# A four-sublayer transformer kernel: the ternary FFN runs once over 512 tokens, and its two square weights share one buffer

## The chip, the cores and the metric

The kernel runs on one core of one Trainium2 chip, in one launch. The metric is the device time of that launch in microseconds, as a median over runs. A run's time is that of the whole launch; the profile shows one execution, and its span reaches from the first to the last instruction.

## The reference

The input x is 16 sequences (tiles) of 512 tokens with 256 features. Four sublayers follow each other, each on a layer norm of x and added back to x:

```python
x = x + L0_attn(layernorm(x))   # linear attention: phi(q) (phi(k)^T v), 16 heads, output projection
x = x + L0_ffn(layernorm(x))    # h = silu(x w1) * (x w2); h = gelu(h h1); h = gelu(h h2); h w3
x = x + L1_attn(layernorm(x))   # softmax(q k^T / 16) v, one head of 256, output projection
x = x + L1_ffn(layernorm(x))    # tanh(x W A1 A2 + bias)
```

The hidden width of L0_ffn is 1024: w1 and w2 are 256 x 1024, h1 and h2 are 1024 x 1024, w3 is 1024 x 256. These five weights hold only -1, 0 and 1, with one scale for each output column.

## The kernel before

Precision: a float32 product is made of fp32r matmuls. An operand is split into a high part (`_hi`) and the rest (`_lo`). The ternary weights are exact in the high part, so an FFN product takes two matmuls (weight x hi, weight x lo); all other products take three (`product3`).

Work is written as steps. A step has a kind, a number and an owner (the letter ahead of the colon), and each engine has its own queue of steps, written out by hand in `PE_ORDERS`, `DVE_ORDERS`, `ACT_ORDERS` and `POOL_ORDERS`, with a part FIRST (the start and tile 0), a part BODY that is walked 14 times, and a part END. `a` and `b` behind a step cut it in two, so that other steps come between. An engine does its queue strictly in order. The engines meet through semaphores: `full` and `taken` of the four PSUM banks in each of two rings (`ffn_fill` for the FFN, `att_fill` for the rest), and counters such as `ffn_ready`, `xt_lo_ready`, `xn_ready`.

The steps that matter here:
- AST, BST, CST, DST: layer-norm statistics on DVE (bn_stats, bn_aggr, adding epsilon), with the inverse root on POOL (L631). ANO, BNO, CNO, DNO: the normalisation on DVE (L686).
- T: DVE transposes the normalised tile by 32 x 32 blocks into `turned` (L764), ACT copies it to `xt_hi` (L953), POOL subtracts to `xt_lo` (L654). LT does the same through TensorE (L1136), ACT (L949) and DVE (L754). NT and NTL are the DVE transposition of half a tile for the FFN (L779, L961, L786).
- U0 to U3 (w1, w2, silu, product), G0 to G3 (h1, gelu), H0 to H3 (h2, gelu), W (w3): the FFN for half a tile of 256 tokens. One step makes two blocks of 128 hidden columns, each 256 tokens wide, in one bank. So a tile takes two passes, and in BODY there are two runs of U, G, H and W: one of the second half of a tile, one of the first half of the next.
- AKV, AS, AQ, AM, AO: the linear attention. Owner `a`.
- CV, CZ, CS0 to CS3, CP0 to CP3, CO0 to CO3, CF: the softmax attention and the last sublayer. CS is a product of scores, then a row maximum on DVE (L869), two small operations (L872, L875), and an exponential on ACT (L1009). CP transposes the probabilities on TensorE (L1252). Owner `c`.

TensorE fills a bank for G or H with 32 matmuls of 256 columns (`hidden`, L1117); U takes 32 for its two banks (`product`, L1048); W is 32 matmuls of 256 columns (L1174). The next layer waits block by block: G0 (and H0, W) waits for `ffn_ready` of the block pair that it reads. All five weights stay in SBUF for the whole run. x has four slots.

ACT's gelu, exponential and silu stand in different tables. Where the function changes, the compiler puts an ACT_TABLE_LOAD ahead of the ACTIVATE.

Of the kernel before, what the change touches and what calls it, by code (L numbers as in the profile page):

```python
# [136 lines left out]
def steps_from(plan):  # L137
# [13 lines left out]
    U0 c:CST U1 U2 U3 c:CNO G0 c:LT c:CB c:CQ G1 c:CV c:CZ G2 c:CS0 G3 c:CP0 c:CS1 c:CS2 c:CO0 c:CP1 c:CS3  # L151
    H0 c:CO1 c:CP2 H1 c:CO2 BST1 c:CP3 BNO1 a:AST H2 c:CO3 c:DST H3 NT1 NTL1 c:DNO W0 c:LT a:ANO U0 U1 c:CF a:T
    U2 U3 a:AB a:AKV0 a:AKV1 a:AKV2 G0 a:AKV3 G1 G2 a:AS a:AQ a:AM G3 a:AO H0 H1 n:BST0 n:BNO0 H2 H3 n:NT0 n:NTL0
    W1""")
# [65 lines left out]
def before(value):  # L220
# [5 lines left out]
    WARM24 p:AST p:ANO p:AB PREP0 p:LT p:AKV0 SCALE p:AKV1 p:AKV2 p:AKV3 PREP1 p:AS f:FA0 p:AQ a:AST f:FA1 p:AM f:FA2  # L226
    f:TA0 p:AO a:ANO a:LT LOOK00 LOOK01 f:TA1 m:BST0 a:AKV0 a:AKV1 f:TA2 m:BNO0 m:BT0 CHECK0
    U0 U1 U2 U3 LOOK10 a:AB LOOK11 a:AKV2 LOOK12 a:AKV3 LOOK13 CHECK1 a:AS a:AQ
    G0 a:AM G1 a:AO WIDE G2 LOOK20 LOOK21 FOLD0 TAKE0 G3 LOOK22 LOOK23 CHECK2 LOOK30
    H0 CHECK3 H1 BST1 BNO1 H2 H3 BT1 W0 U0 U1 U2 U3 G0 G1 G2 G3 H0 H1 n:BST0 n:BNO0 H2 H3 n:NT0 n:NTL0 W1""")  # L230
BODY = PLAN
END = steps_from("""
    U0 U1 U2 U3 G0 G1 G2 G3 H0 H1 BST1 BNO1 H2 H3 BT1 W0 U0 U1 U2 U3 G0 G1 G2 G3 H0 H1 c:CST c:CNO H2 c:LT H3 c:CB W1
    d:CST c:CQ c:CV c:CZ d:CNO d:LT c:CS0 c:CS1 d:CB d:CQ d:CV c:CP0 c:CO0 d:CZ c:CP1 c:CO1 c:CS2 c:CS3
    d:CS0 d:CS1 c:CP2 c:CO2 c:CP3 c:CO3 d:CP0 d:CO0 c:DST d:CS2 d:CP1 d:ES0 d:CO1 d:EN0 c:DNO d:CS3 d:ET0 c:LT d:ES1 d:EN1
    d:CP2 d:EF0 c:CF d:CO2 d:ET1 d:EF1 d:ES2 d:CP3 d:EN2 d:CO3 d:ES3 d:ET2 d:EF2 d:EN3 d:ET3 d:EF3""")


def order_from(plan):
# [21 lines left out]
    p:AST p:ANO PREP0 p:LT p:AKV0 SCALE p:AKV1 p:AKV2 a:ASTa p:AKV3 a:ASTb PREP1 f:TA0 p:AS p:AQ p:AM LOOK00  # L261
    a:ANO LOOK01 p:AO a:LT m:BST0 f:TA1 CHECK0 m:BNO0 f:TA2 a:AKV0 m:BT0 a:AKV1 a:AKV2 a:AKV3 U0 LOOK10
    LOOK11 LOOK12 a:AS LOOK13 a:AQ CHECK1 U1 U2 a:AM U3 a:AO LOOK20 WIDE G0 LOOK21 G1 LOOK22 LOOK23 TAKE0
    CHECK2 LOOK30 G2 G3 CHECK3 BST1 BNO1 H0 H1 n:BST0 H2 H3 BT1 W0 U0 U1 U2 U3 n:BNO0 n:NT0a G0 n:NT0b G1 G2
    n:NTL0 G3 H0 H1 H2 H3 W1"""),
# [5 lines left out]
    "END": order_from("""  # L271
    U0 U1 U2 U3 G0 G1 G2 G3 BST1 BNO1 H0 H1 H2 H3 BT1 W0 U0 U1 U2 U3 G0 G1 G2 G3 c:CST c:CNO H0 c:LT H1 c:CQ
    H2 H3 W1 d:CST c:CV d:CNO c:CZ d:LT c:CS0 c:CS1 d:CQ c:CP0 d:CV d:CZ c:CO0 c:CP1 d:CS0 c:CO1 c:CS2 c:CS3
    d:CS1 c:CP2 d:CP0 c:CO2 c:CP3 d:CO0 d:CS2 d:ES0 c:CO3 d:CP1 c:DSTa d:EN0 c:DSTb d:CO1 d:CS3 d:ET0 d:ES1
    d:CP2 d:EN1 c:DNO d:EF0 d:CO2 d:ET1 c:LT d:CP3 d:EF1 d:ES2 c:CF d:EN2 d:CO3 d:ES3 d:ET2 d:EN3 d:EF2
    d:ET3 d:EF3"""),
# [1092 lines left out]
```

## Time and profile before

| what | value |
|---|---|
| median of 3 runs | 1983.03 us (1981.29 to 1983.25) |
| span of the profiled execution | 1981.5 us |
| mean granted TensorE clock | 0.996 |
| busy: PE, DVE, ACT, POOL | 1961.9, 1289.0, 1020.0, 406.8 us |
| one walk of BODY | 120.64 us |
| DMA moved, mean | 46.03 MB, 23 GB/s |

The profile has no time of its own for the profiled launch besides the span; the span is 1.5 us under the median of the runs. In rows, times are microseconds from the start of the span. Matmuls overlap in their records, so the spacing of matmuls is read from the chain, which counts no microsecond twice.

### The profile page before, as it was taken

To read this page: it belongs to the slowest core of one execution; us is meant where nothing else is said; L and a number is where in the kernel's file an instruction comes from. 1 tells how busy PE (TensorE), PEld (TensorE's weight loads), DVE (VectorE), ACT (ScalarE), POOL (GpSimd) and SP (SyncE) were. 2 spreads that over 40 slices of the span, in tenths; PEclk is the share of its full clock that TensorE was granted. 3 is DMA by queue.
4 is the path that set the end of the run, shared out by engine and by line. 5 is a ranking of instruction groups with operands and counts; after the bars stand their busy time and mean duration, and the time that the engine had idled before them with its cause. 6 is when DMAs were issued, how large, how long until landed. Compare 5 with 4: busy or idle time off the path is not lost.

```text
span 1981.5 us, 37810 instructions
## 1 busy us (share of the span) xinstructions
PE 1961.9 (99%) x15288; PEld 1895.6 (96%) x15288; DVE 1289.0 (65%) x3292; ACT 1020.0 (51%) x1786; POOL 406.8 (21%) x344
## 2 busy tenths in 40 slices
...
DMA packets 24538, 46.03 MB, mean 23 GB/s; under 512 B 1264, under 2 KB 21488, under 8 KB 24176
## 3 DMA queue, kind: packets, MB, share of 16 engines
...
## 4 chain that ended last, share of the span: by engine, by line
PE 97%; DMA 1%; DVE 1%; SPq 1%; issue 0%; ACT 0%; POOL 0%; DVEq 0%; ACTq 0%
PE ffn_fill L1117 49%; PE att_fill L1048 25%; PE ffn_fill L1048 13%; PE ffn_fill L1174 6%; PE att_fill L1136 1%; PE att_fill L1252 1%; DMA scratch_w2T<-in_w2T 1%; DMA w<-scratch_w1T 0%; SPq L543 0%; PE ffn_fill L1285 0%; DVE late_sm L869 0%; PE ffn_fill L1280 0%; ACT late_kv_b L1009 0%; DVE st L671 0%; DVE late_prob_t_lo L864 0%
## 5 line engine op out<-in xcount | busy, mean ns | idle before, releaser
L1117 PE MATMUL ffn_fill<-act_hi,h 128*128 128x256 f32 x4096 | 987.2, 283 | 0.8 <-issue 0.2
L1117 PE MATMUL ffn_fill<-act_lo,h 128*128 128x256 f32 x4096 | 978.2, 280 | 1.2 <-issue 1.2
L1117 PEld LDWEIGHTS ffn_fill<-act_hi,h 128*128 128x128 f32 x4096 | 770.3, 188 | 9.2 <-POOL act_lo L649 3.9
L1117 PEld LDWEIGHTS ffn_fill<-act_lo,h 128*128 128x128 f32 x4096 | 773.1, 189 | 3.6
L976 ACT ACTIVATE whole<-ffn_fill,scales 128x256 f32<-128x256 f32 x512 | 214.0, 469 | 291.3 <-PE ffn_fill L1117 290.1
L649 POOL TENSOR_TENSOR act_lo<-whole,act_hi 128x512 fp32r<-128x512 f32 x128 | 166.8, 1303 | 492.4 <-DVE act_hi L798 492.4
L802 DVE TENSOR_TENSOR act_lo<-whole,act_hi 128x512 fp32r<-128x512 f32 x256 | 183.4, 716 | 112.0 <-ACT act_hi L980 109.7
L1048 PE MATMUL ffn_fill<-half_hi,w 128*128 128x256 f32 x1024 | 245.9, 283 | 0.0
L1048 PE MATMUL ffn_fill<-half_lo,w 128*128 128x256 f32 x1024 | 244.3, 281 | 0.0
L1048 PEld LDWEIGHTS ffn_fill<-half_lo,w 128*128 128x128 f32 x1024 | 193.3, 189 | 0.1
L1048 PEld LDWEIGHTS ffn_fill<-half_hi,w 128*128 128x128 f32 x1024 | 192.5, 188 | 0.4 <-issue 0.2
L631 POOL TENSOR_TENSOR rstd_B<-var_eps_B,minus_half 128x2 f32<-128x2 f32 x32 | 27.8, 868 | 776.4 <-DVE var_eps_B L680 776.4
L967 ACT ACTIVATE gated<-ffn_fill,scales 128x256 f32<-128x256 f32 x256 | 107.3, 471 | 140.4 <-PE ffn_fill L1048 137.3
L980 ACT ACTIVATE act_hi<-whole 128x512 fp32r<-128x512 f32 x256 | 161.9, 633 | 8.1
L976 ACT ACT_TABLE_LOAD x102 | 130.9, 1283 | 59.7 <-PE ffn_fill L1117 58.7
L779 DVE STREAM_TRANSPOSE turned_b<-xn_b 32x128 f32<-32x128 f32 x464 | 140.4, 303 | 6.5
L793 DVE SCALAR_TENSOR_TENSOR whole<-ffn_fill,scales,gated 128x256 f32<-128x256 f32 x256 | 111.8, 478 | 50.3 <-PE ffn_fill L1048 29.3
L1174 PE MATMUL ffn_fill<-w,act_hi 128*128 128x256 f32 x512 | 121.2, 280 | 0.0
L1174 PE MATMUL ffn_fill<-w,act_lo 128*128 128x256 f32 x512 | 120.9, 279 | 0.0
L764 DVE STREAM_TRANSPOSE turned<-xn 32x256 f32<-32x256 f32 x224 | 97.5, 435 | 2.9
L1174 PEld LDWEIGHTS ffn_fill<-w,act_lo 128*128 128x128 f32 x512 | 96.5, 188 | 0.0
L671 DVE BATCH_NORM_STATS2 st<-x 128x6 f32<-128x256 f32 x252 | 92.7, 415 | 5.8 <-DMA x<-in_L_attn_x 4.3
...
## 6 DMA issues: line engine op xcount, KB each, us to landing
x<-in_L_attn_x SPq DMA_DIRECT2D x16, 512.0 KB, 3.3
out<-x SPq DMA_DIRECT2D x15, 512.0 KB, 2.9
...
```

The lines of the kernel that those rows point to most:

```text
L649: pool.tensor_tensor(act_lo[0][:, blocks], whole[:, n % WHOLES], act_hi[0][:, blocks].bitcast(F32), ALU.subtract).then_inc(s["ffn_ready"], 1)
L671: last = dve.bn_stats(st[:, b, :], xs[:, b, :])
L764: last = dve.transpose(into[:, :, :, here:here + SQ], own.xn[here:here + SQ].rearrange("p b (k n) -> p b k n", k=KD) [:, :, :, there:there ...
L779: last = dve.transpose(into[:, :, :, here:here + SQ], xn_b[here:here + SQ].rearrange("p b (k n) -> p b k n", k=KD) [:, :, :, there:there + ...
L793: last = dve.scalar_tensor_tensor(whole[:, n % WHOLES, o, :], two(bank)[:, o, :], scales[:, 1, 2 * j + o:2 * j + o + 1], gated[:, j % 2, o ...
L802: dve.tensor_tensor(act_lo[dst][:, blocks], whole[:, n % WHOLES], act_hi[dst][:, blocks].bitcast(F32), ALU.subtract).then_inc(s["ffn_ready ...
L967: last = act.activation(gated[:, j % 2, o, :], two(bank)[:, o, :], ACT.Silu, scale=scales[:, 0, 2 * j + o:2 * j + o + 1])
L976: last = act.activation(whole[:, n % WHOLES, o, :], two(bank)[:, o, :], ACT.Gelu, scale=scales[:, layer, 2 * j + o:2 * j + o + 1])
L980: act.activation(act_hi[1 if kind == "G" else 0][:, 2 * j:2 * j + 2], whole[:, n % WHOLES], ACT.Copy)\
L1048: last = pe.matmul(out, lhsT, rhs, start=n == 0, stop=n == len(pairs) - 1)
L1117: last = pe.matmul(two(bank)[:, o, :], view(w), view(moving[:, k, :]), start=k == 0 and o == 0 and half == 0, stop=k == KH - 1 and half == ...
L1174: last = pe.matmul(bank[:, 0:D], view(part_of[:, k, b * P:(b + 1) * P]), view(w3[:, k, :]), start=k == 0 and half == 0, stop=k == KH - 1 a ...
```

## The change

The FFN of a tile runs once over 512 tokens. U, G and H have eight steps each; a step makes one block of 128 hidden columns, 512 tokens wide, with matmuls of 512 columns. W stays as it is, as W0 and W1 back to back. `h1` and `h2` no longer lie side by side in SBUF. One buffer `hw` of eight chunks holds one of them; when TensorE has filled G_j's bank, SP loads chunk j of h2 into its place, and behind H_j chunk j of h1. x has three slots instead of four. The probabilities, w3 and some raw weights lie elsewhere, with two pads of eight elements. All queues are new, SP has one of its own, and a walk of BODY now begins in the middle of layer H. ACT's U0 and U1 have one wait more, since W's product now goes through `gated`.

```diff
-SLOTS = 4
+SLOTS = 3
 PE_ORDERS "BODY"
-    U0 U1 U2 U3 G0 G1a c:LT G1b c:CV c:CZ G2a c:CS0 G2b G3a c:CP0 c:CS1 c:CS2 G3b c:CO0 c:CP1 c:CS3 H0a
-    c:CO1 c:CP2 H0b c:CO2 c:CP3 H1 c:CO3 H2 H3 W0 U0 c:LT U1 U2 U3 c:CFa G0a c:CFb G0b G1 G2 G3 a:AKV0
-    a:AKV1 a:AKV2 a:AKV3 H0a a:AS a:AQ a:AM H0b H1a a:AO H1b H2 H3 W1"""),
+         H5 H6 H7 W0 W1 U0 a:AKV0 U1 a:AKV1 U2 a:AKV2 U3 a:AKV3 U4 U5 a:AS a:AQ U6 a:AM U7 G0a a:AO G0b c:LT G1a
+    c:CV     G1b c:CZ G2 c:CS0 G3a c:CP0 c:CS1 c:CS2 G3b c:CO0 c:CP1 c:CS3 G4a c:CO1 c:CP2 G4b c:CO2 c:CP3 G5
+    c:CO3 G6     G7a c:LT G7b H0a c:CFa H0b c:CFb H1 H2 H3 H4"""),
 DVE_ORDERS "BODY"
-    c:CSTa U0 U1 U2 U3 c:CSTb c:CNO c:LT c:CQ c:CV c:CZ c:CS0 G0 c:CP0 c:CS1 c:CS2 c:CO0 G1 c:CP1 c:CS3 G2
-    G3 c:CO1 c:CP2 c:CO2 BST1 c:CP3 H0 BNO1 a:AST c:CO3 c:DSTa H1 c:DSTb NT1a H2 NT1b H3 NTL1 c:DNO W0 U0 U1
-    c:LT U2 U3 a:ANO c:CF a:Ta a:Tb G0 G1 a:AKV0 a:AKV1 G2 a:AKV2 a:AKV3 a:AS G3 a:AQ a:AM a:AO n:BST0 H0
-    n:BNO0 H1 n:NT0a H2 n:NT0b H3 n:NTL0 W1"""),
+         H5 a:AST H6 a:ANO a:Ta H7 a:Tb W0 W1 c:CSTa U0 a:AKV0 U1 a:AKV1 c:CSTb U2 a:AKV2 U3 a:AKV3 U4 U5 a:AS
+    a:AQ U6 a:AM U7 c:CNO a:AO n:BST0 c:LT c:CQ G0 n:BST1 c:CV G1 c:CZ c:CS0 G2 c:CP0 c:CS1 c:CS2 c:CO0 G3
+    c:CP1 c:CS3 c:CO1 c:CP2 G4 c:CO2 c:CP3 n:BNO0 c:CO3 G5 c:DSTa c:DSTb n:NT0a G6 c:DNO n:NT0b c:LT G7 n:NTL0
+    n:BNO1     c:CF H0 n:NT1a H1 n:NT1b H2 n:NTL1 H3 H4"""),
 ACT_ORDERS "BODY"
-    U0 U1 U2 U3 c:LT G0 G1 c:CV c:CZ c:CS0 c:CP0 G2 c:CS1 c:CS2 c:CP1 G3 c:CS3 c:CP2 H0 c:CP3 H1 H2 H3 NT1
-    U0 U1 c:LT U2 U3 c:CF G0 a:T G1 G2 a:AKV0 a:AKV1 a:AKV2 a:AKV3 G3 a:AQ a:AM H0 H1 H2 H3 n:NT0"""),
+         H5 H6 H7 a:T U0 a:AKV0 U1 a:AKV1 U2 a:AKV2 U3 a:AKV3 U4 U5 a:AQ U6 a:AM U7 G0 c:LT G1 c:CV c:CZ G2
+    c:CS0 c:CP0 c:CS1 c:CS2 G3 c:CP1 c:CS3 c:CP2 G4 c:CP3 G5 G6 c:LT n:NT0 G7 H0 c:CF H1 H2 n:NT1 H3 H4"""),
 POOL_ORDERS "BODY"
-    U0 U1 U2 U3 c:CST c:CB BST1 a:AST c:DST U0 U1 U2 U3 c:CF a:T a:AB n:BST0"""),
+         a:AST a:AB a:T U0 U1 c:CST U2 U3 U4 U5 U6 U7 n:BST0 c:CB n:BST1 c:DST c:CF"""),
+SP_ORDERS "BODY"
+    H5 H6 H7 G0 G1 G2 G3 G4 G5 G6 G7 H0 H1 c:CF H2 H3 H4"""),
...
-        h1 = sb("h1", [P, KH, HID], F32R)
-        h2 = sb("h2", [P, KH, HID], F32R)
+        hw = sb("hw", [P, KH, KH, P], F32R)
...
+            def land_chunk(name, j):
+                sp.dma_start(hw[:, j].rearrange("p k n -> p (k n)").bitcast(F32), a["scratch_" + name][j])\
+                  .then_inc(h_loaded[j], 16)
...
+                if kind in ("G", "H"):
+                    b, n = c.bank("ffn_fill", 0)
+                    sp.wait_ge(full["ffn_fill"][b], n)
+                    land_chunk("h2T" if kind == "G" else "h1T", j)
...
+                elif kind == "CF":
+                    t = c.now.get("out_ready", 0)
+                    sp.wait_ge(s["out_ready"], t + 1)
                     sp.dma_start(x_out[t], x[:, t % SLOTS]).then_inc(x_stored, 16)
+                    if t + SLOTS < T:
+                        sp.wait_ge(x_stored, 16 * t + 16)
+                        sp.dma_start(x[:, t % SLOTS], x_in[t + SLOTS]).then_inc(x_loaded[t % SLOTS], 16)
...
                 elif kind == "U":
                     if j >= 2:
                         wait_taken(act, c, "ffn_fill", -3)
+                    else:
+                        wait(act, s["b_done"], c.value("b_done", j - 1))
                     bank, out = filled(act, c, "ffn_fill", 0)
-                    for o in range(2):
-                        last = act.activation(gated[:, j % 2, o, :], two(bank)[:, o, :], ACT.Silu,
-                                              scale=scales[:, 0, 2 * j + o:2 * j + o + 1])
-                    last.then_inc(out, 1)
+                    act.activation(gated[:, j % 2], bank[:], ACT.Silu, scale=scales[:, 0, j:j + 1]).then_inc(out, 1)
...
-            def hidden(c, layer, weights, src, j, piece):
+            def hidden(c, layer, src, j, piece):
                 bank, done = begun(c, "ffn_fill", piece)
+                if piece != "b":
+                    pe.wait_ge(h_loaded[j], weights_loaded(c))
                 def emit(view):
                     for k in halves(piece, KH):
-                        if j == 0 and k % 2 == 0:
-                            pe.wait_ge(s["ffn_ready"], c.value("ffn_ready", k // 2 + 1 - PAIRS))
-                        for o in range(2):
-                            w = weights[:, k, (2 * j + o) * P:(2 * j + o + 1) * P]
-                            for half, moving in enumerate((act_hi[src], act_lo[src])):
-                                last = pe.matmul(two(bank)[:, o, :], view(w), view(moving[:, k, :]),
...
+                        if j == 0:
+                            pe.wait_ge(s["ffn_ready"], c.value("ffn_ready", k + 1 - KH))
+                        for half, moving in enumerate((act_hi[src], act_lo[src])):
+                            last = pe.matmul(bank[:], view(hw[:, j, k, :]), view(moving[:, k, :]),
+                                             start=k == 0 and half == 0, stop=k == KH - 1 and half == 1)
```

In FIRST, tile 0 now has both m:BT0 and m:BT1 (transposition through TensorE for the FFN) ahead of U0, with m:BT1 directly ahead of it.

## Rows read from the trace of the kernel before

**Rows 1.** The page, busy time: us, share of the span, instructions.
```profile
PE 1961.9 (99%) x15288; PEld 1895.6 (96%) x15288; DVE 1289.0 (65%) x3292; ACT 1020.0 (51%) x1786; POOL 406.8 (21%) x344
```

**Rows 2.** Stretches: one walk of BODY, and a part of END; PEclk is the granted clock.
```profile
300.00:420.64 120.64, 120.61 (x950) 117.05 (x949) 80.81 (x208) 64.28 (x112) 25.82 (x21) 1.00 0.03 10
...
1919.00:1945.00 26.00, 24.73 (x151) 21.36 (x149) 21.39 (x54) 11.27 (x21) 6.02 (x5) 1.00 0.00 1
```

**Rows 3.** The chain in BODY, in order of time: start, us, what, matmuls.
```profile
340.50 13.25 PE ffn_fill L1117 x112
353.74 5.60 PE att_fill L1048 x24
...
373.35 9.46 PE ffn_fill L1117 x80
382.80 3.73 PE ffn_fill L1174 x32
...
400.07 0.87 PE att_fill L1136 x8
...
410.31 1.43 PE att_fill L1048 x6
```

**Rows 4.** The timeline, DVE: start, us, line, operation.
```profile
310.44 0.16 DVE L881 RECIPROCAL sm<-sm 128x1 f32<-128x1 f32 x1 [1.79 <-PE att_fill L1048]
...
311.04 0.74 DVE L671 BATCH_NORM_STATS2 st<-x 128x6 f32<-128x256 f32 x2
...
314.20 1.40 DVE L671 BATCH_NORM_STATS2 st<-x 128x6 f32<-128x256 f32 x4
...
316.12 0.16 DVE L881 RECIPROCAL sm<-sm 128x1 f32<-128x1 f32 x1
...
319.37 2.50 DVE L779 STREAM_TRANSPOSE turned_b<-xn_b 32x128 f32<-32x128 f32 x8
321.89 0.69 DVE L802 TENSOR_TENSOR act_lo<-whole,act_hi 128x512 fp32r<-128x512 f32 x1
...
326.48 1.37 DVE L686 TENSOR_SCALAR xn<-x,mv_C,rstd_C 128x256 f32<-128x256 f32 x4
...
341.14 7.17 DVE L764 STREAM_TRANSPOSE turned<-xn 32x256 f32<-32x256 f32 x16
```

**Rows 5.** The timeline, ACT and DVE, behind the last H step of a pass.
```profile
382.90 0.84 ACT L976 ACTIVATE whole<-ffn_fill,scales 128x256 f32<-128x256 f32 x2 [2.28 <-PE ffn_fill L1117]
383.77 0.63 ACT L980 ACTIVATE act_hi<-whole 128x512 fp32r<-128x512 f32 x1
...
384.44 0.69 DVE L802 TENSOR_TENSOR act_lo<-whole,act_hi 128x512 fp32r<-128x512 f32 x1 [0.53 <-ACT act_hi L980]
```

**Rows 6.** The timeline, ACT and POOL, behind the transposition T.
```profile
348.35 1.16 ACT L953 ACTIVATE xt_hi<-turned 128x512 fp32r<-128x512 f32 x2 [3.08 <-DVE turned L764]
...
349.06 2.54 POOL L654 TENSOR_TENSOR xt_lo<-turned,xt_hi 128x512 fp32r<-128x512 f32 x2 [5.36 <-ACT xt_hi L953]
```

**Rows 7.** The timeline, ACT and DVE, behind c:LT.
```profile
400.55 1.09 ACT L949 ACTIVATE xt_hi<-att_fill 128x512 fp32r<-128x512 f32 x2 [6.45 <-PE att_fill L1136]
...
401.25 1.29 DVE L754 TENSOR_TENSOR xt_lo<-att_fill,xt_hi 128x512 fp32r<-128x512 f32 x2 [1.73 <-ACT xt_hi L949]
```

**Rows 8.** The timeline, DVE and ACT, behind c:CS0.
```profile
411.77 0.69 DVE L869 TENSOR_REDUCE sm<-att_fill 128x1 f32<-128x512 f32 x1 [1.76 <-PE att_fill L1048]
...
412.99 1.28 ACT L1009 ACT_TABLE_LOAD   x1 [3.83 <-DVE sm L875]
414.28 0.69 ACT L1009 ACTIVATE kv_b<-att_fill,sm 128x512 f32<-128x512 f32 x1
```

**Rows 9.** Groups of ACT by line, 300 to 1800 us: busy, mean ns, idle before and releaser.
```profile
L976 ACT ACT_TABLE_LOAD x87 | 111.6, 1283 | 36.4 <-PE ffn_fill L1117 35.6
```

**Rows 10.** DMA issues: operation and count, KB each, us from issue to landing.
```profile
x<-in_L_attn_x SPq DMA_DIRECT2D x16, 512.0 KB, 3.3
```

**Rows 11.** The chain while the weights still land.
```profile
44.96 3.84 PE ffn_fill L1048 x32
```

More of the change, by code:

```diff
@@ L46 @@
 HB = HT // P
-PAIRS = KH // 2
-SLOTS = 4
+SLOTS = 3
 WHOLES = 2
@@ L150 @@
 PLAN = steps_from("""
[L151 to L154, printed above, removed]
+    H5 a:AST H6 H7 a:ANO W0 a:AB a:T W1 U0 c:CST a:AKV0 U1 a:AKV1 U2 a:AKV2 U3 a:AKV3 U4 U5 a:AS a:AQ U6 a:AM U7
+    c:CNO a:AO n:BST0 G0 c:LT G1 G2 G3 G4 G5 c:CB c:CQ n:BST1 c:CV c:CZ c:CS0 c:CP0 c:CS1 c:CS2 c:CO0 c:CP1
+    c:CS3 c:CO1 c:CP2 c:CO2 c:CP3 n:BNO0 c:CO3 c:DST n:NT0 G6 c:DNO c:LT G7 n:NTL0 n:BNO1 c:CF H0 n:NT1 H1 H2
+    n:NTL1 H3 H4""")
 def only(*whose):
     return [s for s in PLAN if s[2] in whose]
-CHECKED = ["w12", "h1", "h2", "w3"]
+CHECKED = ["w12", "h1", "h2a", "h2b", "h2c", "h2d", "w3"]
+H1, H2 = CHECKED.index("h1"), CHECKED.index("h2a")
 def total(steps):
@@ L225 @@
 FIRST = steps_from("""
[L226 to L230, printed above, removed]
+    WARM24 p:AST p:ANO p:LT PREP0 p:AKV0 p:AKV1 SCALE p:AKV2 a:AST p:AKV3 f:FA0 PREP1 p:AB p:AS f:TA0 p:AQ p:AM
+    LOOK00 f:FA1 a:ANO LOOK01 p:AO a:LT m:BST0 f:FA2 m:BST1 f:TA1 m:BNO0 a:AKV0 CHECK0 f:TA2 m:BT0 m:BNO1 a:AKV1
+    a:AKV2 a:AKV3 m:BT1 U0 LOOK10 U1 U2 LOOK11 a:AS LOOK12 a:AQ LOOK13 U3 a:AB U4 U5 CHECK1 a:AM U6 WIDE U7 a:AO
+    n:BST0 G0 n:BST1 G1 G2 LOOK20 G3 n:BNO0 FOLD0 TAKE0 G4 CHECK2 LOOK30 G5 n:NT0 G6 CHECK3 LOOK40 n:NTL0 G7
+    n:BNO1 H0 CHECK4 LOOK50 LOOK60 H1 CHECK5 H2 CHECK6 n:NT1 H3 n:NTL1 H4""")
 BODY = PLAN
 END = steps_from("""
[L233 to L236, printed above, removed]
+    o:H5 o:H6 o:H7 o:W0 o:W1 U0 U1 U2 U3 U4 U5 U6 U7 G0 G1 G2 G3 G4 G5 G6 G7 H0 H1 H2 c:CST H3 c:CNO H4 H5 c:LT
+    H6 H7 c:CB W0 W1 d:CST c:CQ c:CV c:CZ d:CNO d:LT c:CS0 c:CS1 d:CB d:CQ d:CV c:CP0 c:CO0 d:CZ c:CP1 c:CO1
+    c:CS2 c:CS3 d:CS0 d:CS1 c:CP2 c:CO2 c:CP3 c:CO3 d:CP0 d:CO0 c:DST d:CS2 d:CP1 d:ES0 d:CO1 d:EN0 c:DNO d:CS3
+    d:ET0 c:LT d:ES1 d:EN1 d:CP2 d:EF0 c:CF d:CO2 d:ET1 d:EF1 d:ES2 d:CP3 d:EN2 d:CO3 d:ES3 d:ET2 d:EF2 d:EN3
+    d:ET3 d:EF3""")
 def order_from(plan):
@@ L260 @@
     "FIRST": order_from("""
[L261 to L265, printed above, removed]
+         p:AST p:ANO PREP0 p:LT p:AKV0 SCALE p:AKV1 p:AKV2 a:ASTa p:AKV3 a:ASTb PREP1 f:TA0 p:AS p:AQ p:AM
@@ L266 @@
+    LOOK00     a:ANO LOOK01 p:AO a:LT m:BST0 m:BST1 f:TA1 CHECK0 m:BNO0 f:TA2 a:AKV0 m:BT0 m:BNO1 a:AKV1 a:AKV2
+    a:AKV3 m:BT1     U0 LOOK10 U1 U2 LOOK11 a:AS LOOK12 LOOK13 a:AQ U3 U4 U5 CHECK1 a:AM U6 WIDE U7 a:AO n:BST0
+    n:BST1 G0 G1 G2 LOOK20     G3 TAKE0 n:BNO0 G4 CHECK2 LOOK30 G5 n:NT0a G6 CHECK3 LOOK40 n:NT0b n:NTL0 n:BNO1
+    G7 CHECK4 LOOK50 LOOK60 H0     CHECK5 CHECK6 n:NT1a H1 n:NT1b H2 n:NTL1 H3 H4"""),
     "BODY": order_from("""
-    c:CSTa U0 U1 U2 U3 c:CSTb c:CNO c:LT c:CQ c:CV c:CZ c:CS0 G0 c:CP0 c:CS1 c:CS2 c:CO0 G1 c:CP1 c:CS3 G2
@@ L271 @@
+    n:BNO1     c:CF H0 n:NT1a H1 n:NT1b H2 n:NTL1 H3 H4"""),
     "END": order_from("""
[L272 to L275, printed above, removed]
@@ L276 @@
-    d:ET3 d:EF3"""),
+         o:H5 o:H6 o:H7 o:W0 o:W1 U0 U1 U2 U3 U4 U5 U6 U7 G0 G1 G2 G3 G4 G5 G6 G7 H0 H1 H2 c:CST H3 c:CNO H4 H5
+    c:LT H6     c:CQ H7 W0 W1 d:CST c:CV d:CNO c:CZ d:LT c:CS0 c:CS1 d:CQ c:CP0 d:CV d:CZ c:CO0 c:CP1 d:CS0
+    c:CO1 c:CS2 c:CS3     d:CS1 c:CP2 d:CP0 c:CO2 c:CP3 d:CO0 d:CS2 d:ES0 c:CO3 d:CP1 c:DSTa d:EN0 c:DSTb d:CO1
+    d:CS3 d:ET0 d:ES1     d:CP2 d:EN1 c:DNO d:EF0 d:CO2 d:ET1 c:LT d:CP3 d:EF1 d:ES2 c:CF d:EN2 d:CO3 d:ES3
+    d:ET2 d:EN3 d:EF2     d:ET3 d:EF3"""),
@@ L292 @@
     "FIRST": order_from("""
-    p:AST a:AST p:AB m:BST0 U0 U1 U2 U3 a:AB BST1 U0 U1 U2 U3 n:BST0"""),
+         p:AST a:AST p:AB m:BST0 m:BST1 U0 U1 U2 a:AB U3 U4 U5 U6 U7 n:BST0 n:BST1"""),
     "BODY": order_from("""
-    U0 U1 U2 U3 c:CST c:CB BST1 a:AST c:DST U0 U1 U2 U3 c:CF a:T a:AB n:BST0"""),
+         a:AST a:AB a:T U0 U1 c:CST U2 U3 U4 U5 U6 U7 n:BST0 c:CB n:BST1 c:DST c:CF"""),
     "END": order_from("""
-    U0 U1 U2 U3 BST1 U0 U1 U2 U3 c:CST d:CST d:CB c:CB d:ES0 c:DST d:ES1 d:EF0 d:EF1 d:ES2 c:CF d:ES3 d:EF2
+         U0 U1 U2 U3 U4 U5 U6 U7 c:CST d:CST d:CB c:CB d:ES0 c:DST d:ES1 d:EF0 d:EF1 d:ES2 c:CF d:ES3 d:EF2
     d:EF3"""),
+}
+SP_ORDERS = {
+    "FIRST": order_from("""
+    G0 G1 G2 G3 FOLD0 G4 G5 G6 G7 H0 H1 H2 H3 H4"""),
+    "BODY": order_from("""
+    H5 H6 H7 G0 G1 G2 G3 G4 G5 G6 G7 H0 H1 c:CF H2 H3 H4"""),
+    "END": order_from("""
+    o:H5 o:H6 o:H7 G0 G1 G2 G3 G4 G5 G6 G7 c:CF d:EF0 d:EF1 d:EF2 d:EF3"""),
 }
@@ new lines, in _ @@
+            sp.dma_start(x[:, 1], x_in[1]).then_inc(x_loaded[1], 16)
+            bounce(w12_bounced, "w1T")
+            bounce(w12_bounced, "w2T")
+            bounce(h1_bounced, "h1T", 0)
+            sp.wait_ge(w12_bounced[0], 16 * 2)
+            land(w12_loaded[0], "w1T", w12[:, 0])
+            land(w12_loaded[1], "w2T", w12[:, 1])
+            bounce(h1_bounced, "h1T", 1)
+            for half in range(2):
+                sp.wait_ge(h1_bounced[half], 16)
+                for j in range(half * KH // 2, (half + 1) * KH // 2):
+                    land_chunk("h1T", j)
@@ L702, in part @@
                     wait(dve, s["turned"], c.value("turned"))
-                    normalise(c, own, x[:, slots[who]], own.xn, "A" if kind == "ANO" else "E" if who == "d" else "C", NB)
+                    stage, of_kind = ("A", "AST") if kind == "ANO" else ("E" if who == "d" else "C", "CST" if kind == "CNO" else "DST")
+                    normalise(c, own, x[:, slots[who]], own.xn, stage, pow_of(c, own, of_kind, 0, who), range(NB))
                 elif kind == "CQ":
@@ L717, in part @@
                     wait_apart(dve, taken[own.ring][b], n)
-                    statistics(c, own, x[:, slots[who]], stage_of(step), NB, share)
+                    statistics(c, own, x[:, slots[who]], stage_of(step), range(NB), share)
                 elif kind == "ES":
```

316 lines of the change are left out of this document (157 added, 159 removed).

## Prediction

> **What bounds the kernel now.** I read the page first: TensorE is busy 1961.9 of 1981.5 us, and no other engine is over 65% [rows 1]. Then the stretches: in one walk of BODY TensorE is busy 120.61 of 120.64 us at a granted clock of 1.00, its upper level of 2.4 GHz [rows 2]. So 14 x 120.64 = 1689 us of the span hold no wait of TensorE at all. Two things can move the time: what a matmul costs, and whether the new queues let TensorE wait. The chain gives the first, the timeline of the other engines the second. The sum is made against the span, 1981.5; the runs' median is 1.5 us above it, and I add that at the end. A difference under 0.2%, 4 us, can't be told from none.
>
> **The matmuls.** 112 matmuls of 256 columns take 13.25 us, 118.3 ns each; 24 of 512 columns take 5.60 us, 233.3 ns each [rows 3]. Two narrow ones cost 236.6 ns, so the change saves 3.3 ns for each wide one. A tile has 64 + 128 + 128 = 320 of these (U, G, H): 1.05 us a tile, 16.7 us for 16 tiles. W is unchanged. The bounds: W's 32 matmuls of 256 columns take 3.73 us, 116.6 ns each [rows 3], which is half of 233.3. So the 1.7 ns that G pays over W may not be the price of a short matmul but of where its operands lie, and may stay at 512 columns. Then the gain is 0. I take 16.7, because the only rows with 512 columns show 233.3, and keep 0 for the range. The Trainium skill ("TensorE: Matmul & The Clock Gate", section "Wait — 56ns, not 53.3ns?") gives each warm matmul a fixed cost of about 2.5 ns; by it the gain would be an estimated 16 x 320 x 2.5 = 12.8 us, 4 less.
>
> **ACT, DVE, POOL: the same elements in fewer instructions.** A gelu that was two records in 0.84 us [rows 5] becomes one of 512 columns; the exponential of 512 columns takes 0.69 [rows 8]. All of this lies under TensorE's matmuls and is worth nothing by itself; it shortens the way from a full bank to DVE's subtraction from 384.44 - 382.81 = 1.63 us [rows 3, 5] to 1.48.
>
> **SP and the chunks.** 16 loads of 512 KB a tile, where x's of that size lands in 3.3 us [rows 10]. A chunk is needed eight steps later, at least 8 x 3.73 = 30 us: hidden. x's load now waits for c:CF and the store, after H1 in SP's queue, behind which only loads of chunks wait. It lands before the walk ends, and a:AST needs it 5.2 us into the next: hidden too, at three slots. Bound: while the weights landed, U's matmuls took 3.84 / 32 = 120.0 ns [rows 11], 1.4% more. If that is the DMA's doing, and a chunk is on its way for 16 x 3.3 = 53 us of a walk, it costs 0.7 us a tile, 12 us in all. I take 0.
>
> **The queues.** Without waits a walk lasts 120.64 - 1.05 = 119.6 us. A G or H step is 16 x 233.3 ns = 3.73 us, half of one 1.87, a U step 1.87. I followed the new queues through BODY with durations from the rows, and find four places where TensorE gets there first:
>
> 1. *a:T before AKV0.* Count from the start of H5. TensorE comes to AKV0 after H5, H6, H7, W0, W1, U0: 5 x 3.73 + 1.87 = 20.5. H6 is full at 7.47, its subtraction starts at 8.95. Behind it DVE has the subtraction (0.69), a:ANO (1.37), Ta (half of 7.17), H7 (0.69) and Tb [rows 4], all in order: 18.9. From T's end to xt_lo ACT and POOL take 351.60 - 348.31 = 3.3 us [rows 4, 6]. AKV0 can start at 22.2. **1.6 us**, half of which shows already in W0, which needs H7's block at 14.5 and gets it at 15.3. W's own two steps on DVE, the release of U0's banks, c:CST and U0 are queued behind Tb and still make it. Before, four G steps lay between T and AKV0.
> 2. *G0 ahead of c:LT on ACT.* Count from G0's full bank, where TensorE starts c:LT. ACT's wait for the bank stands ahead of its table load [rows 9], so G0 takes load 1.29, gelu 0.71, copy about 0.6 [rows 5, 8]: c:LT's copy starts at 2.7. From there DVE starts 0.70 later and gives the first bank back after 0.65 more [rows 7]: 4.05. TensorE has LT (0.87) and G1a (1.87) to do, 2.74, then CV. **1.3 us.** Behind c:LT on ACT stand only G1 and CV.
> 3. *One half step between CS0 and CP0.* From CS0's end (411.74) to the exponential's end (414.97) the row maximum, the table load and the exponential take 3.23 us [rows 3, 8]. Before, G2b and G3a covered it with 3.78; now G3a alone with 1.87. **1.4 us.**
> 4. *DNO before the second c:LT.* Count from CO3's end. DVE: CO3 0.64, G5 0.69, c:DST 1.92, n:NT0a 2.52, G6 0.69, DNO 1.37 [rows 4], 7.8 in all, and 0.2 for the last two transposes: 8.05. TensorE: G6, G7a, LT, 6.47 [rows 3]. **1.6 us.** n:NT0b and c:LT's subtraction wait behind DNO on DVE; CFa, which needs them, comes 0.9 us after.
>
> Elsewhere the walk fits: AM to AO, CP to CO, G7 to H0, the H steps with n:NT1. All four are in places where the waited-for engine is not busy on average, so nothing is given back. Sum: 5.9 us a walk, 14 walks, 82.9 us. Bounds: 0 if each chain is shorter than I read it; one more place like these, 1.4 x 14 = 20 us.
>
> For places 2 and 3 the table load matters. The rows have it at 1.28, and the exponential starts 1.29 after it began [rows 8]. The Trainium skill ("ScalarE: Activation LUTs", section "What ACT_TABLE_LOAD costs") adds about 1380 ns of drain to each switch; places 2 and 3 would then last 2 x 1.38 us longer, 39 us over the run, a time of about 2089. The row has no room for that drain, so I go by the row.
>
> **FIRST and END.** m:BT1 directly ahead of U0 shows its way through ACT and DVE once: about 0.67 + 0.69 = 1.4 us [rows 5]. The other steps of FIRST and END are the same work on TensorE, without attention beside most of it; 0, and 5 us either way for the range.
>
> **Sum.** 1981.5 - 16.7 + 82.9 + 1.4 = 2049.1 span; with 1.5 around it 2050.6 us. Slower by 3.4%.
>
> **Rivals.**
> - *The table loads go ahead of the wait in the new queues* (the compiler places them). Then places 2 and 3 shrink by 1.28 each to about 0.1 and nothing: 2050.6 - 14 x 2.6 = 2014 us. Against it: G's and CS's waits are as they were, and 35.6 of the 36.4 us of idle time ahead of gelu's loads is put down to TensorE [rows 9]. 0.13.
> - *The wait chains overlap more than I read*, because every block could be handed on before its step ends, and the places together cost under (16.7 - 1.4) / 14 = 1.1 us a walk: from there on the kernel is faster. At 0 it gives 1968 us. For it: rows of DVE overlap by up to 0.08 us, which takes some 0.1 off each place; against it: that is far from 1.5. 0.09.
> - *The wide matmuls are quicker in the FFN than in AKV*, where hi and lo weights alternate. From 220 ns down they pay for all waits (5120 of them, 84.3 us); at N / 2.4 GHz plus 2.5 ns, 215.8, the gain is 320 x 20.8 ns = 6.7 us a tile, 107 us: 1961 us. That this is what 512 columns take is the rule of the same TensorE page. Against it: AKV's are 233.3 at the same granted clock [rows 2, 3], and the narrow ones are as far above the rule (118.3). 0.04.
> - *Nothing gained by width, or the chunks' DMA slows the matmuls, or one more place.* 2067 to 2083 us. For it: W's 116.6 and rows 11. 0.19.
> - *The waits lower TensorE's clock.* In END it stood idle for 1.3 of 26 us at a granted clock of 1.00 [rows 2]; waits of 1.3 to 1.6 us are of that order. It would go far above 2083. 0.02.
> - *The change does nothing*, since waits and gain cancel: the narrow zone around 1.1 us a walk. 0.03.
>
> **How the numbers follow.** My forecast, the four places at 1.0 to 1.7 us each with the full gain, has 0.50, and 2030 to 2062 as its own range. Faster: 0.09 + 0.04 = 0.13. Same: 0.03. Slower: 0.84. The range takes in the table-load rival at the bottom and the bounds of width and DMA at the top, and leaves out the faster cases and the clock: 2008 to 2080.
>
> **What would show it.** In the page: TensorE busy about 83 us less than the span beyond the old 20, and its waits on POOL xt_lo, on DVE xt_lo (CV), on ACT kv_b (CP0) and on DVE xn (LT), 14 times each. The spacing in U, G, H at 233.3 ns and half as many matmuls there. In the stretches a walk of 125.5 us. If the walk is 119 to 121 us with no such waits, my following of the queues failed; if waits stand there but at a third of the size, the durations did; if the spacing is not 233, the first term.

## The result, and the profile after

The changed kernel takes 2039.53 us (4 runs, 2039.30 to 2040.71) beside 1983.14 us for the kernel before in the same runs: 2.85% slower, 95% interval 2.7% to 3.0%. The forecast was 2050 us in 2008 to 2080. The span of the profiled execution is 2037.9 us. Two single executions were far slower at a granted clock of 0.72 and 0.70 (one of the kernel before, 2462.69 us, and one of e8, 3391.75 us) and count nowhere here.

The page of the changed kernel, busy time (us, share of the span, instructions) and the DMA issues:

```profile
PE 1926.6 (95%) x10170; PEld 1632.2 (80%) x10170; DVE 1328.5 (65%) x3183; ACT 817.7 (40%) x1286; POOL 409.8 (20%) x344
...
hw<-scratch_h1T SPq DMA_DIRECT2D x128, 512.0 KB, 3.3
hw<-scratch_h2T SPq DMA_DIRECT2D x128, 512.0 KB, 3.2
```

TensorE is busy 35 us less than in [rows 1] and yet the span is 56 us longer: its idle time went from 20 to 111 us. So the loss is waiting, 91 us more of it, less the 35 us of work saved. Who it waited for (line of the waiting matmul, releaser, us in total, times, longest):

```profile
PE att_fill L1170 <- DVE xn L720: 24.5, 16, 4.2
PE att_fill L1283 <- ACT kv_b L1044: 22.3, 15, 1.6
PE att_fill L1083 <- DVE xt_lo L791: 20.2, 15, 1.4
PE att_fill L1083 <- POOL xt_lo L686: 14.2, 14, 1.0
PE ffn_fill L1205 <- DVE act_lo L840: 13.1, 14, 0.9
```

These are the four places of the prediction: c:LT for DNO, CP0 for the exponential of CS0, CV for c:LT's xt_lo, and AKV0 for T, the last with its forerunner in W0. Each stands there 14 times, once for each walk of BODY, or once or twice more: the 4.2 us of the first line, for one, fell in FIRST. Two walks of BODY in a row (stretch, us; busy time of PE, PEld, DVE, ACT, POOL; granted clock, DMA share, GB/s):

```profile
899.60:1024.60 125.00, 118.74 (x629) 100.64 (x629) 83.17 (x201) 50.66 (x80) 26.04 (x21) 1.00 0.23 76
1024.60:1149.60 125.00, 118.76 (x629) 100.62 (x629) 83.13 (x201) 50.64 (x80) 26.03 (x21) 1.00 0.23 76
```

A walk takes 125.00 us instead of 120.64 [rows 2], with 6.2 us of idle TensorE where there were 0.03. The granted clock stayed at 1.00 with these waits in the walk. The same walk in the timeline of TensorE, only the matmuls that waited (start, duration, in brackets the idle time ahead):

```profile
933.98 0.38 PE L1083 MATMUL att_fill<-wvo_hi,xt_hi 128*128 128x256 f32 x1 [1.34 <-DVE xt_lo L791]
...
949.97 0.33 PE L1283 MATMUL att_fill<-ident,kv_b 128*128 128x128 f32 x1 [1.57 <-ACT kv_b L1044]
...
978.01 1.31 PE L1170 MATMUL att_fill<-ident,xn 128*128 128x128 f32 x8 [1.39 <-DVE xn L720]
...
1017.25 0.39 PE L1205 MATMUL ffn_fill<-w,act_hi 128*128 128x256 f32 x1 [0.94 <-DVE act_lo L840]
...
1024.60 0.50 PE L1083 MATMUL att_fill<-wkv_hi,xt_hi 128*128 128x512 f32 x1 [1.02 <-POOL xt_lo L686]
```

They sum to 6.26 us. DVE's queue ahead of the last two shows place 1 as it was followed:

```profile
1010.90 0.69 DVE L840 TENSOR_TENSOR act_lo<-whole,act_hi 128x512 fp32r<-128x512 f32 x1 [1.00 <-ACT act_hi L1015]
1011.50 1.38 DVE L720 TENSOR_SCALAR xn<-x,mv_A,rstd_A 128x256 f32<-128x256 f32 x4
1012.91 3.58 DVE L801 STREAM_TRANSPOSE turned<-xn 32x256 f32<-32x256 f32 x8
1016.50 0.69 DVE L840 TENSOR_TENSOR act_lo<-whole,act_hi 128x512 fp32r<-128x512 f32 x1
1017.23 3.60 DVE L801 STREAM_TRANSPOSE turned<-xn 32x256 f32<-32x256 f32 x8
```

H6's subtraction starts at 1010.90, then a:ANO, Ta, H7, Tb end at 1020.83, and POOL gives xt_lo back 3.7 us later. For place 2, ACT behind G0's full bank:

```profile
930.00 1.28 ACT L1013 ACT_TABLE_LOAD   x1 [6.68 <-PE ffn_fill L1152]
931.29 0.69 ACT L1013 ACTIVATE whole<-ffn_fill,scales 128x512 f32<-128x512 f32 x1
932.01 0.63 ACT L1015 ACTIVATE act_hi<-whole 128x512 fp32r<-128x512 f32 x1
932.55 1.06 ACT L988 ACTIVATE xt_hi<-att_fill 128x512 fp32r<-128x512 f32 x2
```

ACT had been idle for 6.68 us, and the table load still came only behind the bank, which was full at 929.93; c:LT's copy starts 2.62 us after that, against the 2.7 of the forecast.

What the prediction did not have is the pace of the matmuls. The chain of the changed kernel (start, us, what, matmuls):

```profile
938.89 2.72 PE att_fill L1083 x12
...
946.63 0.70 DVE sm L908
947.36 0.23 DVE sm L911
947.61 0.17 DVE sm L914
947.85 1.28 ACT L1044
949.14 0.79 ACT kv_b L1044 x2
949.97 0.66 PE att_fill L1283 x4
...
956.61 0.44 PE att_fill L1283 x4
...
978.01 1.31 PE att_fill L1170 x8
...
987.63 21.80 PE ffn_fill L1152 x96
```

96 matmuls of H1 to H6 take 21.80 us: 227.1 ns each, not 233.3 [rows 3]. CZ's 12 take 2.72, 226.7 ns, and nothing in the order or width of CZ's matmuls was changed.

Behind a wait the chain gives a group of matmuls more time than without one: CP0's four transposes take 0.66 us after the wait for ACT, and those of CP1 at 956.61 take 0.44. The ends of matmul records are modelled, so how this splits into waiting and slow work is rough; the starts are not, and from start to start AKV0's first matmul takes 0.33 us and the second 0.24:

```profile
1024.60 0.50 PE L1083 MATMUL att_fill<-wkv_hi,xt_hi 128*128 128x512 f32 x1 [1.02 <-POOL xt_lo L686]
1024.93 0.40 PE L1083 MATMUL att_fill<-wkv_lo,xt_hi 128*128 128x512 f32 x1
1025.17 0.39 PE L1083 MATMUL att_fill<-wkv_hi,xt_lo 128*128 128x512 f32 x1
```

c:LT's eight transposes take 1.31 us instead of 0.87 [rows 3] for another reason: in the kernel each pair of them waits for its own quarter of DNO, and DVE was still at work on these while TensorE transposed:

```profile
977.46 1.38 DVE L720 TENSOR_SCALAR xn<-x,mv_C,rstd_C 128x256 f32<-128x256 f32 x4
978.01 1.31 PE L1170 MATMUL att_fill<-ident,xn 128*128 128x128 f32 x8 [1.39 <-DVE xn L720]
```

DNO ends at 978.84, and the last pair can't start before that. So c:LT waits for DNO by 0.44 us more than the 1.39 that stand in brackets.

### The profile page after: what moved, and what is told of

It reads as the page before. It is cut to its first block, busy times and chain, and to the rows that moved or that the text cites. A ratio compares the mean times of both kernels' runs of the same rounds, so it can differ in the third digit from the quotient of the medians.

```text
span 2037.9 us, 27407 instructions
## 1 busy us (share of the span) xinstructions
PE 1926.6 (95%) x10170; PEld 1632.2 (80%) x10170; DVE 1328.5 (65%) x3183; ACT 817.7 (40%) x1286; POOL 409.8 (20%) x344
## 2 busy tenths in 40 slices
DMA packets 59241, 171.10 MB, mean 84 GB/s; under 512 B 5296, under 2 KB 25520, under 8 KB 58928
## 4 chain that ended last, share of the span: by engine, by line
PE 76%; DVE 13%; ACT 5%; POOL 2%; issue 2%; DMA 1%; SPq 1%; ACTq 0%; DVEq 0%
PE ffn_fill L1152 37%; PE att_fill L1083 25%; PE ffn_fill L1083 11%; DVE turned L801 5%; POOL xt_lo L686 2%; DVE turned_b L818 2%; DVE act_lo L840 2%; PE att_fill L1283 1%; DVE xn L720 1%; DVE st L704 1%; PE att_fill L1170 1%; ACT whole L1013 1%; ACT L1044 1%; ACT act_hi L1015 1%; ACT L1013 1%
## 5 line engine op out<-in xcount | busy, mean ns | idle before, releaser
L1152 PE MATMUL ffn_fill<-act_hi,hw 128*128 128x512 f32 x2048 | 804.0, 393 | 1.3 <-DVE act_lo L840 1.3
L1152 PE MATMUL ffn_fill<-act_lo,hw 128*128 128x512 f32 x2048 | 798.7, 390 | 0.0
L1152 PEld LDWEIGHTS ffn_fill<-act_hi,hw 128*128 128x128 f32 x2048 | 384.7, 188 | 78.4 <-DVE act_lo L840 1.8
L1152 PEld LDWEIGHTS ffn_fill<-act_lo,hw 128*128 128x128 f32 x2048 | 384.7, 188 | 76.8
L1013 ACT ACTIVATE whole<-ffn_fill,scales 128x512 f32<-128x512 f32 x256 | 175.9, 687 | 526.9 <-PE ffn_fill L1152 526.4
L1083 PE MATMUL ffn_fill<-half_hi,w 128*128 128x512 f32 x512 | 202.6, 396 | 2.3 <-issue 2.3
L1083 PE MATMUL ffn_fill<-half_lo,w 128*128 128x512 f32 x512 | 199.8, 390 | 0.0
L1083 PEld LDWEIGHTS ffn_fill<-half_hi,w 128*128 128x128 f32 x512 | 96.1, 188 | 22.2 <-issue 2.5
L1083 PEld LDWEIGHTS ffn_fill<-half_lo,w 128*128 128x128 f32 x512 | 96.1, 188 | 19.7
L1205 PEld LDWEIGHTS ffn_fill<-w,act_hi 128*128 128x128 f32 x512 | 96.3, 188 | 16.6 <-DVE act_lo L840 16.0
```

The source lines that it names most:

```text
L1013: act.activation(whole[:, n % WHOLES], bank[:], ACT.Gelu, scale=scales[:, layer, j:j + 1]).then_inc(out, 1)
L1083: last = pe.matmul(out, lhsT, rhs, start=n == 0, stop=n == len(pairs) - 1)
L1152: last = pe.matmul(bank[:], view(hw[:, j, k, :]), view(moving[:, k, :]), start=k == 0 and half == 0, stop=k == KH - 1 and half == 1)
L1205: last = pe.matmul(bank[:, 0:D], view(part_of[:, k, tok]), view(w3[:, k, :]), start=k == 0 and half == 0, stop=k == KH - 1 and half == 1)
```

## The experiments

All times are medians of 4 runs (of three for e8), and ratios are against the kernel before, run beside each group (medians 1983.0 to 1985.0 us). Eleven kernels ran.

**Where the 227 ns come from.** The changed kernel has two pads of 8 elements, 32 bytes. The starts of the operands follow from the order and the sizes of the tensors in the kernel. In the kernel before, the start of each weight lies on a multiple of 64 bytes and that of each activation 32 bytes behind one. In the changed kernel the operands of U, G, H, AKV, AQ, CZ and CS all start on a multiple of 64, and w3, wvo, wf, m_parts and the high part of the values 32 bytes off. Run e1 takes the pads out:

```diff
-        sb("beside_0", [P, 8])
-        sb("beside_1", [P, 8])
```

> The changed kernel without its two pads of eight elements. It computes the reference. Theory A: the new kernel's wide matmuls run at 227 ns instead of the 233.3 of before because the pads put both operands of U, G, H, AKV, AQ and CZ in the same half of a 64-byte line; without them one operand lies 32 bytes off, and these go back to 233.3 ns, CO and AO (both operands at 32) to 119.2 ns. That is 5120 + 770 wide matmuls x 6.4 ns = 38 us and 3 us for the narrow ones, less some 12 us because a slower TensorE waits less at two of the four places: about 2068 us. Rival B: 227 ns comes from the width or the order of the steps, not from where the operands lie: 2039 us and 227 ns.

Measured: 2068.47 us, 1.0429 (1.0411 to 1.0448). The chain of e1 has layer H and AO as

```profile
1001.74 22.41 PE ffn_fill L1150 x96
...
938.83 2.86 PE att_fill L1081 x24
```

22.41 / 96 = 233.4 ns, and AO's 24 narrow ones 119.2 ns each. Theory A, and within 1 us of its time.

Run e2 does it to the kernel before:

```diff
+        sb("beside_0", [P, 8])
         scales = sb("scales", [P, 4, KH])
```

> The kernel before with one pad of eight elements ahead of the scales, so that the activations lie on 64-byte lines like the weights. It computes the reference. Theory A: what counts is whether both operands lie in the same half of a line, and it has opposite signs for wide and narrow matmuls: AKV, AQ, CZ go from 233.3 to 227 ns (5 us less), U, G, H from 118.3 to 119.2 ns and W, CV, CF from 116.6 to 119.2 ns (about 14 us more): about 1992 us. Rival B: where operands lie does nothing: 1983 us. Rival C: it is the activations' own place at 32 bytes off a line that costs, at any width: G below 117 ns and 1965 us or less.

Measured: 2000.56 us, 1.0088 (1.0070 to 1.0106). The chain of e2:

```profile
952.19 13.44 PE ffn_fill L1118 x112
965.63 5.47 PE att_fill L1049 x24
```

The 112 narrow matmuls go from 118.3 to 120.0 ns and AKV's 24 wide ones from 233.3 to 227.9, opposite signs as in theory A. The narrow ones lose more than the 0.9 ns that I had put in: 10240 in the FFN x 1.7 ns is 17 us.

Run e9 moves everything by 32 bytes:

```diff
+        sb("ahead", [P, 8])
         w12 = sb("w12", [P, 2, KD, HID], F32R)
```

> The changed kernel with one more pad of eight elements ahead of the first tensor: everything moves by 32 bytes, so that operands which shared the first half of a 64-byte line now share the second. It computes the reference. Theory A (only the distance of the two operands counts): 227 ns in U, G, H and 2039.5 us. Rival B (the absolute place counts, 64-byte alignment is fast): 233 ns and about 2068 us.

Measured: 2040.47 us, 1.0286 (1.0269 to 1.0303), and in its chain

```profile
988.80 21.80 PE ffn_fill L1153 x96
```

227.1 ns. Of A and B it is A: the distance between the two operands counts, and a shift of both by 32 bytes does nothing. How far the rule reaches is not shown. In all these kernels the operands "in the same half" are also a whole number of 256 bytes apart, and the others 32 bytes more or less, so nothing here says that the period is 64 bytes.

The kernel before had one group of wide matmuls of this kind, the scores CS, whose two operands are both activations:

```profile
410.42 0.39 PE L1048 MATMUL att_fill<-xt_lo,qz_hi 128*128 128x512 f32 x1
...
411.34 0.40 PE L1048 MATMUL att_fill<-xt_hi,qz_lo 128*128 128x512 f32 x1
```

These are four matmuls from start to start, 0.92 us, 230 ns each: under 233.3, though not 227.

**Whether the four places are the loss.** Run e3 rearranges the queues there and nowhere else (each line shows one stretch of an engine's queue, before and after, the rest cut):

```diff
 DVE  -H5 a:AST H6 a:ANO a:Ta H7 a:Tb W0            +a:AST H5 a:ANO a:Ta H6 H7 a:Tb W0
      -c:CZ c:CS0 G2 c:CP0 c:CS1 c:CS2 c:CO0 G3     +c:CZ c:CS0 c:CP0 c:CS1 c:CS2 c:CO0 G2
      -c:CP1 c:CS3 c:CO1                            +c:CP1 c:CS3 G3 c:CO1
      -c:DSTb n:NT0a G6 c:DNO n:NT0b c:LT G7        +c:DSTb c:DNO n:NT0a c:LT G6 G7 n:NT0b
 ACT  -U7 G0 c:LT G1 c:CV c:CZ G2 c:CS0 c:CP0       +U7 c:LT G0 c:CV G1 c:CZ c:CS0 c:CP0
      -c:CS1 c:CS2 G3 c:CP1                         +c:CS1 c:CS2 G2 c:CP1 G3
      -G6 c:LT n:NT0 G7                             +G6 c:LT G7 n:NT0
 PE   -c:CZ G2 c:CS0 G3a c:CP0                      +c:CZ G2a c:CS0 G2b G3a c:CP0
```

> The changed kernel with its BODY queues rearranged at the four places only (T ahead of H6 and H7 on DVE with its statistics ahead of H5; c:LT ahead of G0 on ACT; a whole step between CS0 and CP0, with G2 behind CS2 on ACT; DNO ahead of NT0a, and NT0b and n:NT0 behind G7). It computes the reference. Theory: TensorE's 6.2 us of idle time per walk of BODY and the slower first matmuls behind each wait (1.2 us) stand at these places alone, so nearly all of it goes: 14 x 7.2 = 100 us less, 1940 us, below the kernel before, with at most 0.3 us idle per walk. Rival: the engines are late for lack of slack anywhere in the walk, and the waits come back at other steps: 2010 us or more.

Measured: 1942.04 us, 0.9794 (0.9776 to 0.9812): 97.5 us less than the changed kernel, and faster than the kernel before. One walk of e3, and its largest wait:

```profile
974.30:1092.27 117.97, 117.67 (x629) 100.71 (x629) 84.06 (x201) 50.99 (x80) 25.88 (x21) 1.00 0.24 81
...
PE att_fill L1083 <- POOL xt_lo L686: 4.3, 14, 0.6
```

The walk is 7.03 us shorter, with 5.9 us less idle time and 1.1 us less busy time for the same 629 matmuls. Of the latter 0.44 us is c:LT, whose transposes no longer keep pace with DNO (they take 0.87 us in e3's chain); the rest is what the other groups lost behind their waits.

The four places one by one (each from the changed kernel, with the edit of e3 at that place alone; e7 keeps c:LT behind G0 on ACT, e6 keeps `G1 c:CV`):

> The changed kernel with place 1 alone rearranged: on DVE AST ahead of H5, then H5, ANO, Ta, H6, H7, Tb. It computes the reference. Theory (local waits): W0's wait (0.94 us) and AKV0's (1.01 us) go, with the slower first matmuls behind them (0.3 us at AKV0): 14 x 2.2 = 31 us less, 2009 us, and the other three places keep their waits. Rival (one late engine): the time comes back at the other places, 2030 us or more.

> The changed kernel with place 2 alone: on ACT c:LT ahead of G0. It computes the reference. Theory: CV's wait of 1.35 us and 0.27 us behind it go: 14 x 1.6 = 23 us less, 2017 us, the other places unchanged. Rival: 2030 us or more, with the wait now at CZ or CS0.

> The changed kernel with place 3 alone: TensorE does CS0 in the middle of G2, so that a whole step lies between CS0 and CP0; ACT does c:CV ahead of G1, and G2 behind CS2, DVE follows. It computes the reference. Theory: CP0's wait of 1.49 us and 0.22 us behind it go: 14 x 1.7 = 24 us less, 2016 us. Rival: with half a step less between CZ and CS0 the wait goes there (c:LT behind G0 on ACT still delays CV and CZ): 2030 us or more.

> The changed kernel with place 4 alone: on DVE DNO ahead of NT0a, c:LT ahead of G6 and G7, NT0b behind them; on ACT n:NT0 behind G7. It computes the reference. Theory: c:LT's wait of 1.45 us and 0.44 us behind it go: 14 x 1.9 = 26 us less, 2013 us. Rival: the wait goes to CFa or to H0b's block of G7: 2030 us or more.

| run | place | median | less than 2039.5 | ratio (95%) |
|---|---|---|---|---|
| e5 | 1, T before AKV0 | 2013.38 | 26.2 | 1.0150 (1.0133 to 1.0167) |
| e6 | 2, c:LT behind G0 | 2017.37 | 22.2 | 1.0172 (1.0155 to 1.0189) |
| e7 | 3, CS0 to CP0 | 2017.92 | 21.6 | 1.0171 (1.0154 to 1.0188) |
| e8 | 4, DNO behind NT0a | 2015.81 | 23.7 | 1.0160 (1.0140 to 1.0180) |

The sum is 93.7 us, all four together gave 97.5: the waits are local, and none of size comes back elsewhere. The waits of e5, with place 1 rearranged, show the other three untouched:

```profile
PE att_fill L1170 <- DVE xn L720: 24.1, 16, 4.2
PE att_fill L1283 <- ACT kv_b L1044: 21.9, 14, 1.6
PE att_fill L1083 <- DVE xt_lo L791: 20.3, 15, 1.4
PE att_fill L1083 <- POOL xt_lo L686: 4.4, 14, 0.6
```

W0's wait is gone from it, and AKV0's went from 14.2 to 4.4 us, not to 0, which is why e5 brought 26 and not 31.

**The chunks' DMA.** Run e4 reads an eighth of each chunk in every reload:

```diff
+                if not first_of_all[0]:
+                    sp.dma_start(hw[:, j, 0].bitcast(F32), a["scratch_" + name][j][:, 0:P]).then_inc(h_loaded[j], 16)
+                    return
```

> The changed kernel with every reload of a chunk cut to its first 128 of 1024 elements per partition; the h1 and h2 layers then compute with a mixture of weights, everything else is the same. Theory: the chunks' DMA costs nothing, since they land long before they are read and matmuls next to them run as fast as others: 2039 us, 227 ns. Rival: the DMA slows matmuls by the 1.4% seen in the start of the kernel before while it runs (about half the time in layer H): 5 to 12 us less, 2028 to 2035 us.

Measured: 2039.78 us, 1.0287 (1.0268 to 1.0305), 57.33 MB moved instead of 171.10, and in the chain

```profile
987.36 21.80 PE ffn_fill L1158 x96
```

The same 227.1 ns, and no wait of TensorE on a chunk stands in either profile. The chunks' bytes cost nothing; the number of DMA packets stayed at 59241, so what the packets by themselves cost was not tried.

**A better version.** Run e10 adds two edits to e3: each AKV one U step later, and m:BT1 ahead of a:AKV3 in FIRST (TensorE's queue is shown; DVE's and ACT's follow it).

```diff
 PE   -W1 U0 a:AKV0 U1 a:AKV1 U2 a:AKV2 U3 a:AKV3 U4 U5 a:AS    +W1 U0 U1 a:AKV0 U2 a:AKV1 U3 a:AKV2 U4 a:AKV3 U5 a:AS
 PE   -m:BT0 a:AKV2 a:AKV3 m:BT1 U0                             +m:BT0 a:AKV2 m:BT1 a:AKV3 U0
```

> The kernel with the four places rearranged (run e3) and two more edits: in BODY each AKV comes one U step later on all engines, and in FIRST m:BT1 comes ahead of a:AKV3. It computes the reference. Theory: AKV0's remaining wait of 0.3 us and the slower first matmuls behind it (0.3 us) go 14 times, 8 us, and U0's single wait of 2.3 us goes: 1932 us. Rival: W0's release or AS comes too late in the shifted order and the wait only moves: 1940 us.

Measured: 1944.21 us, 0.9805 (0.9788 to 0.9821), 2 us more than e3. The forecast failed and its rival holds: AKV0's wait is gone, and the waits of e10 begin with

```profile
PE att_fill L1083 <- DVE xn L860: 9.1, 14, 0.8
```

This is AS, which now follows AKV3 by one U step of 1.8 us, too little for ACT's and DVE's part of AKV3. So run e11 has `U1 a:AKV0 U2 a:AKV1 a:AKV2 U3 a:AKV3 U4 U5 a:AS`.

> Run e10 showed AKV0's wait gone and a new one of 0.65 us at AS, which came only one U step behind AKV3. Here the order is U1, AKV0, U2, AKV1, AKV2, U3, AKV3, U4, U5, AS on all engines; everything else as in e10. It computes the reference. Theory: AS has two U steps of cover again, and 14 x 0.65 = 9 us and the slow first matmuls behind (0.1 to 0.3 us each) go: 1932 us. Rival: AKV1 and AKV2 back to back or the later U steps find another late engine: 1940 us or more.

Measured: 1933.22 us, 0.9739 (0.9723 to 0.9756), the fastest of all. Its walk has no wait left:

```profile
934.21:1051.54 117.33, 117.31 (x629) 100.82 (x629) 83.78 (x202) 50.92 (x80) 25.86 (x21) 1.00 0.24 81
```

## Why the prediction was right, point by point

The forecast had the cause and the places right: the new queues let TensorE wait at four places, and this outweighs what the wide matmuls save. That it came within 11 us is partly luck. The matmuls were 39 us cheaper than forecast, in the FFN and in the attention together, and what stands behind the waits, with the rest of the account, 28 us dearer. By the prediction's own sign ("if the spacing is not 233, the first term") its first term failed. Run e1, in which the spacing is the 233 that the forecast assumed, took 2068.47 us, 18 more than the 2050.6.

- **The matmuls: 16.7 us forecast, 49 us by the measured pace.** The term that was mis-sized. Width alone did what the row said: without the pads a wide matmul takes 233.4 ns beside twice 118.3, 5120 x 3.2 = 16 us (e1). The pads, which I named in the change and costed at nothing, gave another 6.3 ns each: 5120 x (236.6 - 227.1) = 49 us in all, and some 0.5 us a walk in the attention's products. The bound "it may be where the operands lie" was the right thought with the wrong end: I used it only against the gain. The reason given, that the only rows with 512 columns show 233.3, overlooked CS at 230. The rival of quicker wide matmuls, at 0.04, was set aside because AKV showed 233.3; AKV went to 227 with the FFN. The half steps of G between attention's pieces run at 230 to 232 ns, for which I have no cause.
- **The waits: 5.9 us a walk forecast, 6.7 measured** (6.2 of idle time and 0.44 at c:LT). By place: 1.96 against 1.6, 1.34 against 1.3, 1.57 against 1.4, and 1.39 + 0.44 = 1.83 against 1.6, since the forecast of place 4 had counted to the end of c:LT. In place 2 the terms 1.29, 0.71 and 0.6 add up to 2.6, not the 2.7 that the forecast went on with; measured were 2.62. Place 1 was too small since TensorE came earlier, with faster matmuls, and POOL took 3.0 us instead of 2.5 for its two subtractions. Runs e5 to e8 and e3 show that these are the loss.
- **Behind the other waits: not forecast, some 0.8 us a walk**, 11 us over the run: 0.2 at CP0, 0.3 each at CV and AKV0. In AKV0 0.1 of it shows in the starts of the matmuls, and the rest hangs on modelled ends; why, is open.
- **The account of a walk**: 120.64 + 6.2 (idle) + 1.2 (c:LT and behind the other waits) - 3.0 (FFN) - 0.5 (attention) = 124.5, measured 125.00. About 0.5 us stays open; the half steps are part of it.
- **The table load behind the wait** held in the new queues. The Trainium skill ("ScalarE: Activation LUTs", section "What ACT_TABLE_LOAD costs") adds a drain of about 1380 ns to a load. It does not show here: the load began at 930.00, 0.07 us after the bank was full, and the gelu at 931.29, 1.29 us after the load began. The Trainium skill ("TensorE: Matmul & The Clock Gate", section "Wait — 56ns, not 53.3ns?") has 215.7 ns for 512 columns. No group of wide matmuls in the chains of these runs reached it (227 to 234 ns at a clock of 1.00).
- **The chunks and x's slots: 0 forecast.** The chunks' bytes cost 0 (e4). For x's slots no run was made, but no wait on x stands in BODY.
- **FIRST: 1.4 us forecast for m:BT1**, 2.3 us of wait measured ahead of U0. From m:BT1's full bank at 46.77 to the end of its part on ACT and DVE at 48.27 it is 1.5 us, as forecast; for the other 0.8 the profile shows nothing that TensorE waited for.
